# Boundary sums of V with 128 contraction rows, one more product per chunk on VectorE, and combine weights spread by TensorE

## What is computed

```python
k_w, v_w = windows(k), windows(v)            # 17 x 17 around each pixel, zeros outside the image
attn = softmax(einsum('bhnc,bhnlc->bhnl', q, k_w)) * mask
out = einsum('bhnl,bhnlc->bhnc', attn, v_w) @ w_proj.T + b_proj
x = x + out
t = tokens(x); n = layernorm(t)
rw, re = top_k(softmax(n @ router_w.T), 2); rw = rw / rw.sum()
for e in range(8):                           # combine[:, e] is rw where expert e was picked, else 0
    t = t + combine[:, e:e+1] * (gelu(n @ w1[e] + b1[e]) @ w2[e] + b2[e])
```

## Time and profile before

| | us |
|---|---|
| median of 3 runs | 521.24 (516.85 to 523.06) |
| the profiled execution | 523.58 |
| its span | 521.8 |

### The profile page before, as it was taken

How to read it: one execution, slowest core, us unless ns; L and a number is a source line. 1 busy time by engine, 2 the same in 40 slices (tenths; PEclk the granted TensorE clock), 3 DMA queues, 4 the chain that set the end, 5 groups by cost and what they waited for, 6 DMA issues and landing times.

```text
span 521.8 us, 16704 instructions
## 1 busy us (share of the span) xinstructions
PE 459.8 (88%) x7018; PEld 291.2 (56%) x7018; DVE 305.1 (58%) x763; ACT 275.8 (53%) x485; POOL 214.8 (41%) x263
## 2 busy tenths in 40 slices
PE   4999936599999999999999999669987994999697
PEld 2799914377766777776667776521322451255343
DVE  2330456399998999998888997422234238015233
ACT  2320248588898989999999786210101130034232
POOL 9303260567665655666667673570201005001000
PEclk9775558699999999999999999876856697579989
DMA  6089886456576657666565448770000000000520
GB/s 197 8 287 254 228 290 204 154 191 203 203 222 197 206 180 259 210 206 208 188 199 182 160 163 225 214 221 9 0 1 0 0 2 0 0 16 1 190 83 28
DMA packets 38760, 75.53 MB, mean 145 GB/s; under 512 B 9460, under 2 KB 25733, under 8 KB 37869
## 3 DMA queue, kind: packets, MB, share of 16 engines
q1 hardware_dynamic: 37822, 72.95, 44.4%
q0 software_dynamic: 144, 1.31, 0.7%
q10 hardware_dynamic: 720, 0.22, 0.2%
HBM read 44.08 MB, written 29.26 MB: 141 GB/s over the span
## 4 chain that ended last, share of the span: by engine, by line
PE 80%; issue 6%; DVE 5%; DMA 4%; POOL 2%; ACT 2%; SPq 0%; DVEq 0%; POOLq 0%; ACTq 0%
PE ps L966 19%; PE ps L1058 10%; PE ps L989 9%; PE ps L1011 7%; PE ps L971 6%; PE ps L1161 4%; PE ps L1116 4%; PE ps L931 3%; PE ps L992 3%; PE ps L924 3%; PE ps L997 2%; DVE prb L1429 1%; DMA slabs<-combd 1%; PE ps L887 1%; PE ps L1069 1%
## 5 line engine op out<-in xcount | busy, mean ns | idle before, releaser
L966 PE MATMUL ps<-slabs 128*32 128x401 f32 x528 | 118.9, 515 | 21.2 <-POOL slabs L596 18.6
L966 PE MATMUL ps<-prb,slabs 128*32 128x401 f32 x494 | 115.3, 519 | 0.0
L1355 DVE CUSTOM_DVE_ANT_0 scn<-ps,con 128x401 f32<-128x401 f32 x120 | 64.9, 571 | 31.9 <-PE ps L971 31.7
L770 ACT ACTIVATE exb<-scn,lowest 128x401 f32<-128x401 f32 x120 | 74.2, 621 | 10.6 <-DVE lowest L1355 10.4
L971 PEld LDWEIGHTS ps<-con,slabs 128*32 128x32 f32 x960 | 42.6, 112 | 48.9 <-issue 48.2
L1345 DVE COPY_PREDICATED slabs<-con,zt 128x1152 f32<-128x1152 int32 x41 | 66.7, 1626 | 0.1
L589 POOL TENSOR_TENSOR slabs<-con,qrot 128x192 f32<-128x192 f32 (+4 forms) x67 | 31.3, 471 | 81.4 <-DVE slabs L1345 76.8
L971 PE MATMUL ps<-con,slabs 128*32 128x128 f32 x960 | 62.2, 278 | 0.1
L759 ACT ACTIVATE prb<-slabs 64x1169 f32<-64x1169 f32 x40 | 47.2, 1180 | 13.6 <-DVE slabs L1345 13.0
L989 PE MATMUL ps<-con,exb 128*128 128x128 f32 x360 | 49.3, 281 | 1.0 <-issue 0.5
L1011 PE MATMUL ps<-pm,slabs 128*32 128x78 f32 (+19 forms) x2720 | 48.5, 221 | 0.2 <-DVE osel L1389 0.2
(11 more groups left out here) (161 smaller groups left out, 768.9 us busy)
## 6 DMA issues: line engine op xcount, KB each, us to landing
slabs<-zsl SPq DMA_DIRECT2D x40, 539.5 KB, 3.9
zsl<-uv SPq DMA_DIRECT2D x44, 484.5 KB, 3.6
slabs<-combd SPq DMA_DIRECT2D x2, 1600.0 KB, 8.5
ebs<-zsl SPq DMA_DIRECT2D x4, 539.5 KB, 7.6
slabs<-kimd SPq DMA_DIRECT2D x2, 881.7 KB, 12.0
vimd<-vimg SPq DMA_DIRECT2D x1, 1612.0 KB, 5.6
xt<-x_in SPq DMA_DIRECT2D x8, 200.0 KB, 6.9
kimd<-prb SPq DMA_DIRECT2D x1, 1596.0 KB
```

Of the source, the lines that this page charges most:

```text
L770: nc.scalar.activation(v(ex[x & 1], a, (1, NC3)), v(scn, (x & 1) * NB * NC3 + a, (1, NC3)), ACT.Exp, scale=-1.0, bias=lowest[:, NB * (x & ...
L966: mm(bank(g, (1, NC3), parts=TW, p0=TW * i), w, v((kt, kh)[b & 1][x & 1], b // 2 * C, (1, NC3)), start=first, stop=False, skip_group_check ...
L1355: nc.vector.tensor_tensor_reduce(v(scn, i * NC3, (1, NC3)), bank(g, (1, NC3)), cv("pos"), 1.0, 3e38, ALU.add, ALU.min, lowest[:, i:i + 1]) ...
```

## The change

1. **Sums.** Each member of a group is contracted over all 128 partitions. The weights are now four precomputed tables `slots[j]` (128 x 128, in the free end of `qrot`), in which the rows that don't matter are zero; GpSimd makes them with four multiplications at the end of the loop, of the constant `slot_of` and a new constant `alive`. The unused partitions of `prb` are zeroed at the start (the memset of `kx` becomes one of `prb`, 3200 columns where there were 3192).
2. **Order in a chunk.** The first group starts the bank; `turned_back(k)` comes after the last group and ends it. `attend(k)` waits for it (`nat_done`). The waits for the bank's last reader move from `turned_back` to the first group.
3. **Products.** `VD` is 3, 3, 3, 3: groups (2, 2) and (3, 2) move from GpSimd to VectorE.
4. **Turn.** `turn_out` issues one DMA, which writes both copies, where it issued two.
5. **Combine weights.** Chunk 2's are spread by TensorE as those of chunks 0 and 1 (`BYPE = 3`): 32 transposes more. Only chunk 3's go through DRAM: one DMA of 1600 KB in place of two.

```diff
-VD = (3, 3, 2, 2)
+VD = (3, 3, 3, 3)
+BYPE = 3
+    t["alive"] = p[:, None] // 8 < NCC - np.arange(HC)[None]
+        slots = [v(qrot, L + j * C, (1, C)) for j in range(VGROUPS)]
             def turn_out(a, z, done):
-                for i in range(2):
-                    sp.dma_start(dv(frd, i * C * L + a * Q, (L, C), (1, (z - a) * Q)), frot[:, a * Q:z * Q]).then_inc(done, 16)
+                sp.dma_start(dv(frd, a * Q, (L, C), (C * L, 2), (1, (z - a) * Q)),
+                             v(wide, a * Q, (0, 2), (1, (z - a) * Q))).then_inc(done, 16)
...
-            for k in range(2, NQ):
-                sp.dma_start(v(slabs, (k - 2) * E8 * Q, (Q, E8), (1, Q)),
-                             dv(combd, k * Q, (0, C), (L, E8), (1, Q))).then_inc(weights_in[k - 2], 16)
+            sp.dma_start(v(slabs, 0, (1, E8 * Q)), dv(combd, 0, (0, C), (1, E8 * Q))).then_inc(weights_in, 16)
...
                 if i == SZ - 1:
+                    for j in range(VGROUPS):
+                        gp.tensor_tensor(v(qrot, L + j * C, (TW, VGROUPS), (1, TW)),
+                                         cv("slot_of", (0, VGROUPS), (1, TW), off=24 - 8 * j),
+                                         cv("alive", (VGROUPS, VGROUPS), (0, TW), off=j), ALU.mult
+                                         ).then_inc(S["slots_ready"], 1)
...
                 for m in range(members(j)):
-                    n8 = live(j + VGROUPS * m)
-                    src = v(slabs, late_buf(n) + m * Q, (1, Q), parts=n8) if late else v(pr[n & 1], m * Q, (1, Q), parts=n8)
-                    last = mm(bank(NATB[k], (1, Q), parts=TW, p0=TW * m), cv("slot_of", (1, TW), off=24 - 8 * j, parts=n8), src,
-                              start=False, stop=(j + VGROUPS * (m + 1) >= HC - 1 and j >= 2), skip_group_check=True)
+                    src = v(slabs, late_buf(n) + m * Q, (1, Q)) if late else v(pr[n & 1], m * Q, (1, Q))
+                    last = mm(bank(NATB[k], (1, Q), parts=TW, p0=TW * m), slots[j][:, TW * m:TW * (m + 1)], src,
+                              start=(j == 0), stop=False, skip_group_check=True)
...
             def attend(k):
-                dve.wait_ge(S["vused_late"], vlate(k, VGROUPS - 1) + 1)
+                dve.wait_ge(S["nat_done"], k + 1)
...
             weighted(0, 1)
+            product(2, 2)
             rstd(1)
...
             weighted(0, 6)
+            product(3, 2)
             attend(3)
```

More of the change, by code:

```diff
@@ L295, in program @@
         q_in = [sem(f"q_in{i}") for i in range(2)]
-        weights_in = [sem(f"weights_in{k}") for k in range(2, NQ)]
+        weights_in = sem("weights_in")
         nat_in = [sem(f"nat_in{k}") for k in range(NQ)]
@@ L579, in _ @@
             pool.wait_ge(S["var_ready"], 1)
-            gp.memset(kx, 0.0).then_inc(S["kx_zero"], 1)
+            gp.memset(prb[:], 0.0).then_inc(S["kx_zero"], 1)
             pool.wait_ge(S["qy_ready"], NQ)
@@ L1038, in turned_back @@
             def turned_back(k):
[L1039 to L1043, removed]
                 pe.wait_ge(nat_in[k], 16 * len(TURNED[k]))
-                mm(bank(NATB[k], (1, Q)), cv("perm"), v(sbd, k * Q, (1, Q)), start=True, stop=False, skip_group_check=True)
+                mm(bank(NATB[k], (1, Q)), cv("perm"), v(sbd, k * Q, (1, Q)), start=False, stop=True, skip_group_check=True
+                   ).then_inc(S["nat_done"], 1)
             def vsum(k, j):
@@ L1054, in vsum @@
                     pe.wait_ge(S["vprod"], n + 1)
+                pe.wait_ge(S["slots_ready"], VGROUPS)
+                if j == 0 and k < 2:
+                    pe.wait_ge(S["masked"], SZ)
+                    pe.wait_ge(S["o_used"], SZ)
+                elif j == 0:
+                    pe.wait_ge(S["att_nat"], (1, 3)[k - 2])
                 for m in range(members(j)):
[L1056 to L1059 removed]
+                    src = v(slabs, late_buf(n) + m * Q, (1, Q)) if late else v(pr[n & 1], m * Q, (1, Q))
+                    last = mm(bank(NATB[k], (1, Q), parts=TW, p0=TW * m), slots[j][:, TW * m:TW * (m + 1)], src,
+                              start=(j == 0), stop=False, skip_group_check=True)
                 last.then_inc(S["vused_late" if late else "vused"], 1)
@@ L1124, in spread @@
                     pe.wait_ge(S["att_nat"], 2)
-                elif e == 1:
+                elif e == 1 and k < 2:
                     pe.wait_ge(S["comb_copied"], k + 1)
@@ L1181, in _ @@
             rn_rows(1)
-            turned_back(0)
             vsum(0, 0)
             vsum(0, 1)
-            turned_back(1)
             vsum(0, 2)
             vsum(0, 3)
+            turned_back(0)
             x_part(0)
@@ L1198, in _ @@
             vsum(1, 3)
+            turned_back(1)
             pe.wait_ge(S["w_late"], 16 * 7)
@@ L1201, in _ @@
             up(0, 1)
-            turned_back(2)
             vsum(2, 0)
@@ L1215, in step @@
                 down(k, e)
-                if k < 2 and e + 2 < E8:
+                if k < BYPE and e + 2 < E8:
                     spread(k, e + 2)
@@ L1228, in _ @@
             vsum(2, 3)
+            turned_back(2)
             step(0, 3)
             eb_rows(3)
-            turned_back(3)
             step(0, 4)
@@ L1237, in _ @@
             vsum(3, 3)
+            turned_back(3)
             step(0, 6)
@@ L1263, in _ @@
             for k in range(2, NQ):
+                if k < BYPE:
+                    spread(k, 0)
                 y_start(k)
                 y_bias(k)
+                if k < BYPE:
+                    spread(k, 1)
                 for e in range(E8):
@@ L1513, in weighted @@
                 dve.wait_ge(S["gelu_done"], t + 1)
-                if k < 2:
+                if k < BYPE:
                     dve.wait_ge(S["c_ready"], t + 1)
                 elif e == 0:
-                    dve.wait_ge(weights_in[k - 2], 16)
+                    dve.wait_ge(weights_in, 16)
                 if t >= 2:
                     dve.wait_ge(S["y_done"], t - 1)
-                tt(hw[e & 1], hb[e], bank((6, 4)[e & 1], (1, Q)) if k < 2 else weight_slab(k, e), ALU.mult
+                tt(hw[e & 1], hb[e], bank((6, 4)[e & 1], (1, Q)) if k < BYPE else weight_slab(k, e), ALU.mult
                    ).then_inc(S["weighted"], 1)
```

11 lines of the change are left out of this document (5 added, 6 removed).

## The result

The changed kernel takes 470.4 us, the median of 4 runs (468.8 to 471.4); the one before 520.6, the median of 4 (516.9 to 523.1). The ratio is 0.904, with a 95% interval of 0.898 to 0.910: faster by some 50 us. The profiled execution took 468.8, its span is 467.0. Some executions run in a slower state: ratios are of the others alone, medians of all.

The account below looks back on a forecast made before the run. TensorE was taken to bound the tail after the loop. Stages summed to 456.3 us at full clock, 459.3 with the routing chain, 469.3 with the clock, 471.1 with 1.8 around the span; forecast 471, range 460 to 490.

Parts of the forecast that it names:

- A to G: Stages after the loop, cut at VectorE's closing steps: `attend(0)` to `attend(3)`, `finish(1)`, `finish(2)`, the end; 178 us before.
- E and F: Stages from `attend(3)` to `finish(1)` and on to `finish(2)`; forecast 28.2 and 15.2 us, from 29.8 and 18.8.
- B's work: TensorE's work from `attend(0)` to `attend(1)`: groups, full matmuls, denominators' rows, variance, logits and transposes, together 8.9 us.
- B to D: Stages from `attend(0)` to `attend(3)`; forecast 11.4, 22.4 and 14.7 us at full clock, before additions for routing and clock.
- Groups: Boundary sums on TensorE: 16 groups fall from 2.37 to 0.81 us each at full clock, 37.9 to 13.0 us.
- Stage A: Loop's end to `attend(0)`: groups run before the turned result, landing at 348.7; end at 350.3 in place of 367.4.
- The clock: Half clock on TensorE between the loop's end and `attend(3)`: 10 us added, between nothing and 18 more.
- The routing chain: Chunk 1's chain on VectorE, stalled beside GpSimd between `attend(2)` and `attend(3)`: 3 us added, bounds 0 and 5.8.
- Waits: TensorE waiting for VectorE's products: (1,2) 2.5 us, (2,0) 5.2, (3,0) and (3,1) together 4.5.
- So a group runs nearly serially: Boundary sums before: four matmuls one after another would be 2.68 us; the difference from the scores is contraction rows.
- The rival that the groups stay serial: Boundary sums: something other than rows parts the matmuls; 27 us more, some 35 with half clock, 506 us; chance 0.06.
- The slower rival: TensorE stays at half clock through the whole tail after its first wait; 544 us; chance 0.03.

Follow-up runs that it names:

- turn_two: The changed kernel with the write-out of the loop's result again in two DMAs per piece; 470.2 us, ratio 0.909 to the kernel before.
- fill: The changed kernel with 3, 6 and 6 unread matmuls in TensorE's idle times before groups (1,2), (2,0), (3,1); 462.2 us, ratio 0.891.
- order2: The changed kernel with VectorE making product (2,0) before chunk 0's norm and routing chain, (3,1) straight after (3,0); 455.7 us, ratio 0.878.
- order2_fill: `order2` with three matmuls whose result nobody reads in the idle time before group (1,2); 454.2 us, ratio 0.871.
- order3: `order2` with product (1,2) also ahead of the reciprocal of chunk 0's deviation; 450.8 us, ratio 0.867.
- turn_first: The changed kernel with the turned result again ahead of each chunk's first group; 473.3 us, ratio 0.914.

## Why the prediction was right

**The sum.** Forecast 471.0, measured 470.4. At full clock I had A to G as 6.5, 11.4, 22.4, 14.7 + 3, 28.2, 15.2, 14.1; measured, with the clock in it, 6.5, 15.0, 24.3, 19.2, 27.9, 16.0, 14.1. E and F together are 0.4 off, A and G nothing. (The terms of B's work add up to 8.7 where the sum has 8.9.) The span was forecast at 469.3 and is 467.0: B to D are 3.0 shorter than with the 10 us for the clock, E and F 0.4 and the end of A 0.3 longer. By that account the profiled execution should have taken 471.1, and took 468.8. That the median agrees to 0.6 us is in part luck: it lies 1.6 above the profiled execution, where before's, on which I leaned, lay 2.3 below it.

**Groups.** Priced at 0.81, measured 0.81 at full clock and 1.5 at half.

**Stage A.** First closing step expected to end at 350.3, measured 350.6. The turn landed at 349.1 (expected 348.7): the one larger write-out took 4.75 us of the chain where two took 4.06, the read-back 3.12 for 3.41; `turn_two` shows no difference in total.

**The clock.** I took 10 us over A to D. A is as its sum says; B to D are 58.5 us against 51.5 of my sum with the routing chain's 3, so 7 in place of 10, under half of the 18 that I had as the upper bound. These 7 are what is left over, with the errors of the waits in them; the busy time in the three stretches at half level gives 7.4. The time at half level, by 1 - PEclk of the rows above: 2 x (0.23 x 15.0 + 0.14 x 24.3 + 0.18 x 19.2) = 21 us, where 72 had been. `fill` confirms the price from the other side: with the idle times filled, 8 us went.

**The routing chain.** I added 3 us. By the rows above, the two steps took 1.13 and 0.95 in place of 0.19 each, and a third 0.73: together 2.2 more. The rule of the Trainium skill that I cited (GPSIMD Engine Reference, "Key points") fits again: the step that stood still has two SBUF operands, the product beside it reads PSUM and takes 1.82.

**Waits.** Named for (1,2), 2.5 us, (2,0), 5.2, and (3,0) and (3,1), 4.5 together; measured 2.29, 4.82, and 0.77 + 5.44. These were the right places, as `order2` shows: I left them as they stood, but they were worth 15 us.

**The step that was wrong.** "So a group runs nearly serially", and with it that the number of rows should be 128. The price came out because the new form was priced by rows of its own shape; the reason was wrong: a group ran as three blocks, one for each class of rows, the first with two members together. The line that says so (weight loads in order of time) was in the trace of before. The rival that the groups stay serial was priced from four members, 27 us at full clock and 35 with the clock; the measured return to mixed rows costs 31 with the clock, at 2.37 a group.

**The slower rival.** Nothing like it: PEclk is 1.00 from stage E on. Half clock did stand behind the waits (`order2`, 358 to 368, 0.66), but it came and went: it is some 21 us of stages B to D, as above, where it was 72 of A to D. The rule of the Trainium skill that I cited for this rival (TensorE: Matmul & The Clock Gate, "Why this matters for your kernels") agrees with these rows as to what a gap does: 8 us came back when the gaps were filled.

## What to carry to other kernels

When matmuls into different output slices seem not to overlap, look at the weight loads: those that stand together ran together. Give all members of a group contraction rows of one class by zero weights; here it cost no time (120 rows and 128 agree) and made a group three times as fast. When that is done, the waits between short bursts are next, and a wait can cost twice, once itself and once through half clock behind it: move the producer's instruction ahead of the chain that it merely stands behind (15 and then 5 us here), before touching any work.

## What the runs showed of the hardware

- Members of 120 and 88 rows ran together, and so did 112 and 80, 104 and 72, 120 and 120, 64 and 64; each change of class (72 to 120, 40 to 64, 8 to 32) began a new block of 0.79 us for 400 float32 columns at full clock. A group of 96, 64 and 32 rows costs 2.36, as much as 120, 88, 56 and 24. The prediction had not seen that 120 rows would do as well as 128.
- Fifteen matmuls whose result nobody reads made a kernel 8 us faster (0.891 against 0.904): in `order2` half clock stood behind the 2.29 us idle before 358.46, and with three such matmuls in that place the same ten microseconds ran at 1.00. Idle times of 0.73 and 0.58 us stood ahead of a fall in `order2_fill` (0.52 from 369.0 to 372.5), and 0.74 and 0.58 ahead of none in `order3`.
- A group at half clock takes 1.45 (two in 2.90 in `turn_first`), and 0.81 at full clock: the gain of the new form stays at either level.
